# Attention and mixture-of-experts block: the last two output tiles stored one by one, batch 2's variance and batch 1's last normalisation moved earlier

## What is computed

```
x = x + ln(attention(ln(x)))                 # 4 x 512 x 128, softmax over 512 keys
c = sigmoid(ln(x) @ W_enc + b_enc) @ W_s2c + b_s2c      # 256 wide, then 64
gate = top-2 of softmax(c @ Wr + br), 8 experts, renormalised
m = sum_e gate_e * (relu(c @ W1_e + b1_e) @ W2_e + b2_e)
d = sigmoid(m @ W_c2s + b_c2s) @ W_dec + b_dec          # 128 wide
x = x + ln(layernorm(d) * ln_g + ln_b)
```

## Time and profile before

| | |
|---|---|
| median of 3 executions | 127.52 us (127.51 to 127.85) |
| the profiled execution | 127.50 us, of which the span is 125.7 us |
| busy: PE, DVE, ACT, POOL | 117.3, 92.8, 60.6, 34.6 us |
| granted clock of TensorE over the span | 0.984 of full speed |
| DMA packets | 9372, 12.43 MB |

### The profile page before, as it was taken

One profiled execution on the slowest core, in us unless ns is written; L12 is line 12 of the kernel. 1 busy time (PEld: TensorE's weight loads), 2 busy tenths in 40 slices (PEclk: granted clock), 3 DMA queues, 4 the chain that ended last, 5 costly groups with the idle time before them and its releaser, 6 DMA issues.

```text
span 125.7 us, 2501 instructions
## 1 busy us (share of the span) xinstructions
PE 117.3 (93%) x814; PEld 80.7 (64%) x814; DVE 92.8 (74%) x394; ACT 60.6 (48%) x179; POOL 34.6 (28%) x71
## 2 busy tenths in 40 slices
PE   6999999999999999999999999999999999999900
PEld 2656786778638677754476767776458766966800
DVE  1858896996479625699755868897947999489873
ACT  1647766648746486302556735130565314175430
POOL 4422635242221003305000022460330431224361
PEclk9999999999999999999999999999999999999985
DMA  3548920000000049500000386049500059402022
GB/s 122 125 104 235 207 77 0 0 0 3 0 5 0 5 101 342 229 8 0 0 0 5 101 317 256 9 85 382 216 0 0 5 217 354 190 0 86 0 86 83
DMA packets 9372, 12.43 MB, mean 99 GB/s; under 512 B 3170, under 2 KB 5999, under 8 KB 9359
## 3 DMA queue, kind: packets, MB, share of 16 engines
q1 hardware_dynamic: 8782, 12.14, 29.9%
q10 hardware_dynamic: 576, 0.13, 0.5%
HBM read 11.16 MB, written 1.11 MB: 98 GB/s over the span
## 4 chain that ended last, share of the span: by engine, by line
PE 92%; DVE 2%; ACT 2%; POOL 1%; issue 1%; POOLq 1%; DVEq 0%; ACTq 0%
PE ps_o L828 12%; PE ps_t L940 12%; PE ps_s L803 11%; PE ps_t L815 6%; PE ps_s L917 5%; PE ps_ac L917 5%; PE ps_o L852 3%; PE ps_ac L951 3%; PE ps_ac L1008 3%; PE ps_ac L852 3%; PE ps_ac L870 2%; PE ps_ac L776 2%; PE ps_o L917 2%; PE ps_ac L786 2%; PE ps_t L754 2%; PE ps_t L934 2%
## 5 line engine op out<-in xcount | busy, mean ns | idle before, releaser
L438 POOL TENSOR_TENSOR rstd<-var_eps,minus_half 128x2 f32<-128x2 f32 (+1 forms) x32 | 24.8, 779 | 83.5 <-DVE var_eps L1185 35.9
L828 PEld LDWEIGHTS ps_o<-v,probsT 128*128 128x128 f32 x128 | 15.7, 191 | 3.8 <-ACT probsT L556 3.1
L828 PE MATMUL ps_o<-v,probsT 128*128 128x128 f32 x128 | 17.5, 280 | 0.2 <-ACT probsT L556 0.2
L551 ACT ACTIVATE probs<-ps_s,neg_max 128x512 f32<-128x512 f32 x16 | 11.0, 686 | 11.4 <-DVE neg_max L1208 11.3
L803 PE MATMUL ps_s<-xnT,yT 128*128 128x512 f32 x32 | 16.2, 599 | 0.0
L940 PE MATMUL ps_t<-gated,w 128*64 128x256 f32 x128 | 16.0, 385 | 0.0
L1208 DVE TENSOR_REDUCE neg_max<-ps_s 128x1 f32<-128x512 f32 x16 | 11.0, 687 | 4.8 <-PE ps_s L803 4.6
L940 PEld LDWEIGHTS ps_t<-gated,w 128*64 128x64 f32 x128 | 8.4, 136 | 5.9 <-DVE gated L1302 1.9
L1302 DVE SCALAR_TENSOR_TENSOR gated<-ps_s,b_minus,gate_all 128x512 f32<-128x512 f32 x14 | 9.9, 744 | 1.6 <-PE ps_s L917 0.9
L556 ACT ACTIVATE probsT<-ps_t 128x512 f32<-128x512 f32 x16 | 9.5, 594 | 2.9 <-PE ps_t L815 2.7
L815 PEld LDWEIGHTS ps_t<-ident,probs 128*128 128x128 f32 x64 | 7.3, 141 | 3.9 <-ACT probs L551 1.9
(11 more groups left out here) (206 smaller groups left out, 221.7 us busy)
## 6 DMA issues: line engine op xcount, KB each, us to landing
gate_all<-gates SPq DMA_DIRECT2D x12, 512.0 KB, 6.0
gate_all<-gates SPq DMA_DIRECT2D x8, 256.0 KB, 3.5
x_in<-in_L_attn_x SPq DMA_DIRECT2D x3, 256.0 KB, 3.8
w<-in_L_ffn_W SPq DMA_DIRECT2D x3, 256.0 KB, 4.3
out<-x_out SPq DMA_DIRECT2D x3, 256.0 KB, 2.3
x_in<-in_L_attn_x SPq DMA_DIRECT2D x2, 128.0 KB, 2.4
out<-x_out SPq DMA_DIRECT2D x2, 128.0 KB, 1.7
w_enc<-in_L_ffn_W_enc SPq DMA_DIRECT2D x1, 128.0 KB, 2.6
```

The costliest lines, as they stand in the source:

```text
L438: nc.gpsimd.tensor_tensor(rstd[part], var_eps[part], minus_half[:, t0:t1], ALU.pow).then_inc(g_rstd[n], 1)
L551: nc.scalar.activation(probs[:, b % 2, t], ps_s[:, t % 2], ACT.Exp, bias=neg_max[:, b % 2, t:t + 1], accum_out=prob_sum[:, b % 2, t:t + 1] ...
L828: mm = nc.tensor.matmul(attn_out(t), probsT[:, b % 2, t, k], v[:, b % 2, k], start=(k == 0), stop=(k == T - 1))
```

## The change

Four edits. The last 128 KB store is split: SP stores the fourth tile (64 KB, when all eight v_out of batches 2 and 3 are there), ACT's queue the third (64 KB, at seven). The final wait counts one DMA more. On POOL, `z_add(1)` goes ahead of batch 2's pow. On ACT, `z_norm(1)` goes ahead of `dec_square(2, 0)`. On DVE, `dec_var(2, 0)` goes behind gating 5 instead of gating 6.

```diff
@@ SP
-            for i in range(2):
-                store(B - 1, i)
-            sp.wait_ge(d_out, 16 * parts_done(LN_Z, B - 1, 1))
+            store(B - 1, 0)
+
+            sp.wait_ge(v_out, T * (B - 2))
+            sp.dma_start(out_dram[B - 1, :, T - 1:T], x_out[:, B - 1, T - 1:T]).then_inc(d_out, 16)
+            sp.wait_ge(d_out, 16 * (parts_done(LN_Z, B - 1, 1) + 1))
@@ POOL
             minus_means(1)
+            z_add(1)
             inverse_std(LN_DEC, 2, 0)
-            z_add(1)
             inverse_std(LN_Z, 2, 0)
@@ ACT
+            z_norm(1)
             dec_square(2, 0)
-            z_norm(1)
             moe_out(3)
...
             z_square()
+            act.wait_ge(v_out, T * (B - 2) - 1)
+            act.dma_start(out_dram[B - 1, :, T - 2:T - 1], x_out[:, B - 1, T - 2:T - 1]).then_inc(d_out, 16)
@@ DVE
                 gate_hidden(3, e)
-                if e == 6:
+                if e == 5:
                     dec_var(2, 0)
```

## The result

| | before | after |
|---|---|---|
| median of 5 executions | 127.72 us (127.51 to 127.90) | 125.82 us (125.65 to 126.29) |
| the profiled execution | 127.50 us, span 125.7 | 126.29 us, span 124.5 |

The ratio is 0.9857, with a 95% interval of 0.9833 to 0.9881: 1.4% faster, as forecast, and outside the 0.3% that could be doubted.

What follows compares the result with a forecast made beforehand. From 118 us on, DVE's lateness with batch 2 was taken to set the end, with PE the next limit. 127.50 - 1.50 (order) - 0.15 (stores) = 125.85 us, range 125.5 to 126.5.

Steps and rivals of the forecast that it cites:

- z_norm in ACT's gap, at no cost: On ACT before batch 2's squares: z_norm's 1.65 us fit into 3.00 us of idle time, 0.3 us to spare.
- The addition beside the gatings, at no cost: POOL's addition of batch 1 runs under DVE's gatings 4 and 5 without holding them up; no cost.
- The variance earlier, 0.55 us: On DVE, batch 2's variance one gating earlier ends the pow sooner, so z_scale starts at 112.71 instead of 113.26.
- The collision, 1.00 us: On DVE, z_scale of batch 2 no longer meets POOL's addition and takes 1.14 instead of 2.14 us.
- 1.55 us less 0.05 to PE: At the end, DVE's 1.55 us pass on, but PE's last group takes back 0.05: net gain 1.50 us.
- The stores, 0.15 us: At the end, SP's last store carries 64 KB instead of 128 and lands sooner: gain 0.15 us.
- the sum would have been 126.0: Last stores: 64 KB transfers are mostly overhead, so the split gives nothing; 126.0 us, chance 0.3 within the forecast's 0.80.
- the gatings were not held up: Rival on DVE: POOL's addition holds up gating 4, costing 0.7 us; time 126.65, chance 0.07.
- ACT's store lands before SP's: Rival at the end claimed the reverse: ACT's store lands last, 0.5 us lost; time 126.5, chance 0.06.
- The slower rival: On DVE, the variance waits for late squares and blocks gatings 6 and 7; time 127.9, chance 0.03.
- The sum, 125.85 us: Whole kernel: 127.50 less 1.50 for the order and 0.15 for the stores gives 125.85 us.

Runs made afterwards that it cites:

- norm and addition only: Kernel before with only z_norm(1) on ACT and z_add(1) on POOL moved ahead, variance and stores as before; ratio 0.9909 to the kernel before.
- order only: Kernel before with the three moves on POOL, ACT and DVE but without the split store; ratio 0.9874 to the kernel before.
- both on SP: Kernel after with the third tile's store on SP's queue instead of ACT's; 126.23 us, ratio 0.9885 to the kernel before.
- norm back: Kernel after with z_norm(1) put back behind batch 2's squares on ACT; 127.90 us, ratio 1.0020 to the kernel before.

## Why the prediction was right

- *z_norm in ACT's gap, at no cost*: right. It starts 0.04 us after mean_rstd's end, as 108.15 against 108.11; the squares did not move against gating 4 (0.35 us before it in both).
- *The addition beside the gatings, at no cost*: right, 1.41 us for the pair.
- *The variance earlier, 0.55 us*: measured 0.56. *The collision, 1.00 us*: measured 1.01, and 0.99 by itself in norm and addition only.
- *1.55 us less 0.05 to PE*: right in size. z_last's first half moved by 1.57 us against gating 4, the second by 1.36. The first of the last x_out starts 1.55 earlier, the last ends 1.50 earlier: the 0.05 is the last two tiles' pow, which waits for the statistics of the second half (its pair of pows takes 1.41 instead of 1.36).
- *The stores, 0.15 us*: about 0.1 in the profiles, not to be told from nothing in the time. The landing was 1.6 us, not 1.5. The rule of the Trainium skill (DMA: Bandwidth & Descriptors, "Rules for kernel authors"), by which the sum would have been 126.0, is not refuted by the time: order only, at 126.25 us and 0.9874, lies within the intervals of the whole change. Its words on overhead are on transfers under 64 KB, and these have 64. Its other half, that spreading over engines only saves the sequencer's issue time, agrees with both on SP, where the second issue came 0.13 us later behind the last x_out.
- *One misreading, without effect*: the prediction takes 117.13 for the end of the first tile's squares; it is the end of the second tile's, and so of the whole first half.
- *The rivals*: the gatings were not held up; ACT's store lands before SP's. The slower rival did not come about, but a relative did when it was provoked: a wait at the head of a queue, on POOL and not on DVE, made norm back slower than before.

The sum, 125.85 us, stands 0.03 from the median. Part of that is luck: the kernel before's five executions spread over 0.39 us, and the after's over 0.64.

## What to carry to other kernels

One tile that lasts four times as long as its neighbours is worth a look at what the other engine reads meanwhile: here POOL's addition of two SBUF tensors cost DVE 1 us beside an instruction with two SBUF inputs, and nothing beside one that took one of its two tensors from PSUM. Moving such an addition takes its producer along: with POOL's order changed and ACT's not, the kernel was slower than at the start. And when a wait is won, don't take the next releaser from the name beside the wait alone: compare the gap behind its end with the gap where it really came last, here 0.24 us against 0.03.

## What the runs showed that was not expected

The page of the profile before puts 92% of the chain that ended last on PE. It does not show that at the very end PE's result lay ready for 1.4 us, because DVE had come late from batch 2. In the kernel after, a row names POOL as the releaser of z_last's second half, although POOL's pow had been over for 0.24 us and PE's group ended last. And a pow of POOL that reads SBUF did not hold up a DVE tile with two SBUF tensors, where an addition did.
